# Two experts' reads, a third table and a new order of the first batch in a transformer layer with a mixture of experts

## What is computed

```python
x = x + tanh(g_xattn) * cross_attention(layernorm(x), ctx)   # 16 heads of 8, causal mask
x = x + tanh(g_ffn) * moe(layernorm(x))
# moe: 8 experts, each token takes its best 2
probs = softmax(xt @ Wr);  topv, topi = top_k(probs, 2);  topv /= topv.sum()
rank = cumsum(one_hot(topi), axis=0)          # place of a token with its expert
keep = (rank <= 160) * one_hot(topi)          # 160 = capacity, for each of the two choices
h = gelu(xt @ W1[e] + b1[e]);  y = h @ W2[e] + b2[e]     # 128 -> 512 -> 128, float32
out = sum over the token's kept choices of weight * y[e]
```

## Time and profile before

| | us |
|---|---|
| median of the runs (141.72 to 141.99) | 141.88 |
| the profiled execution | 142.43 |
| its span, first to last instruction | 140.2 |
| PE busy | 122.2 (87%) |
| DVE busy | 103.5 (74%) |
| POOL busy | 83.6 (60%) |
| ACT busy | 74.1 (53%) |
| POOL's 16 sends of rows (L558) | 18.6 |
| POOL's 18 scatters of results (L588) | 19.9 |

### The profile page before, as it was taken

One profiled execution on the slowest core, in us unless ns is written; L12 is line 12 of the kernel. 1 busy time (PEld: TensorE's weight loads), 2 busy tenths in 40 slices (PEclk: granted clock), 3 DMA queues, 4 the chain that ended last, 5 costly groups with the idle time before them and its releaser, 6 DMA issues.

```text
span 140.2 us, 2215 instructions
## 1 busy us (share of the span) xinstructions
PE 122.2 (87%) x698; PEld 85.1 (61%) x703; DVE 103.5 (74%) x262; ACT 74.1 (53%) x135; POOL 83.6 (60%) x125
## 2 busy tenths in 40 slices
PE   5998978999899999896989979969989999989920
PEld 2443844455455656633449647759889999967710
DVE  5599855947584637399569698793699999999290
ACT  4924667166361447335916397671697777811210
POOL 6679779999999140021678658760077877772000
PEclk9999999999999999999999999999999999999996
DMA  3899880003340000000079601113820001101805
GB/s 97 257 217 228 207 274 4 5 0 91 71 140 0 5 0 0 0 0 2 19 222 301 215 22 39 39 53 65 181 66 29 26 31 43 39 30 25 294 0 150
DMA packets 19017, 12.22 MB, mean 87 GB/s; under 512 B 3381, under 2 KB 16999, under 8 KB 19008
## 3 DMA queue, kind: packets, MB, share of 16 engines
q1 hardware_dynamic: 17344, 9.59, 26.7%
q0 software_dynamic: 1088, 1.86, 4.1%
q10 hardware_dynamic: 576, 0.66, 1.3%
HBM read 7.25 MB, written 5.06 MB: 88 GB/s over the span
## 4 chain that ended last, share of the span: by engine, by line
PE 27%; DVE 22%; POOL 17%; issue 15%; DMA 8%; ACT 6%; POOLq 2%; DVEq 0%; SPq 0%
PE turn L870 5%; POOL results L588 5%; DVE top L1319 5%; POOL slots L558 4%; DMA xn_all<-results 3%; PE turn L883 3%; PE av L926 3%; DVE shared L1621 3%; DMA X<-x 3%; POOL shared L479 2%; PE av L934 2%; PE turn L889 2%; DMA results<-p,result_of 2%; PE turn L1105 2%; PE sc L902 2%
## 5 line engine op out<-in xcount | busy, mean ns | idle before, releaser
L1319 DVE TENSOR_REDUCE top<-turn 128x3 fp32r<-128x462 f32 (+2 forms) x44 | 26.2, 606 | 13.6 <-PE turn L870 7.4
L588 POOL DMA_INDIRECT results<-p,result_of x18 | 19.9, 1103 | 13.6 <-DVE p L1604 8.4
L682 ACT ACTIVATE p_all<-sc 128x1024 f32<-128x1024 f32 x16 | 15.5, 1022 | 16.9 <-PE sc L902 16.9
L558 POOL DMA_INDIRECT slots<-rows,slot_of x16 | 18.6, 1164 | 9.3 <-issue 7.3
L870 PE MATMUL turn<-shared,q_all 128*128 128x462 f32 (+2 forms) x44 | 20.3, 468 | 2.3 <-DVE top L1319 0.8
L1196 PE MATMUL sc<-q_all,w_all 128*128 128x320 f32 x96 | 17.4, 320 | 1.1 <-issue 0.7
L756 ACT ACTIVATE late<-sc,B 128x320 f32<-128x320 f32 x32 | 14.9, 522 | 3.0 <-PE sc L1196 3.0
L1196 PEld LDWEIGHTS sc<-q_all,w_all 128*128 128x128 f32 x96 | 14.2, 188 | 2.2 <-issue 1.9
L870 PEld LDWEIGHTS turn<-shared,q_all 128*128 128x128 f32 x44 | 8.3, 189 | 11.2 <-ACT q_pack_all L645 3.8
L1621 DVE TENSOR_TENSOR shared<-late,shared 128x640 fp32r<-128x640 f32 x16 | 13.1, 821 | 0.3
L549 POOL TENSOR_SCALAR_AFFINE_SELECT p_all<-p_all 128x512 f32<-128x512 f32 x7 | 4.5, 644 | 9.5 <-ACT p_all L682 9.5
(11 more groups left out here) (252 smaller groups left out, 280.5 us busy)
## 6 DMA issues: line engine op xcount, KB each, us to landing
W<-w SPq DMA_DIRECT2D x8, 256.0 KB, 3.2
p_all<-w SPq DMA_DIRECT2D x8, 256.0 KB, 4.4
slots<-slot SPq DMA_DIRECT2D x1, 1386.0 KB, 10.6
results<-zeros SPq DMA_DIRECT2D x2, 512.0 KB, 9.3
parts_all<-slots SPq DMA_DIRECT2D x5, 198.0 KB, 3.0
X<-x SPq DMA_DIRECT2D x2, 256.0 KB, 3.6
xn_all<-results SPq DMA_DIRECT2D x2, 256.0 KB, 4.1
xn_all<-results ACTq DMA_DIRECT2D x2, 256.0 KB, 4.3
```

Source lines behind the costliest of these rows:

```text
L558: nc.gpsimd.indirect_dma_start(out=slots, out_offset=bass.IndirectOffsetOnAxis(ap=slot_of[:, c:c + 1], axis=0), in_=rows[:, t, :], in_offs ...
L588: nc.gpsimd.indirect_dma_start(out=results, out_offset=bass.IndirectOffsetOnAxis(ap=result_of[0:m, e, n:n + 1], axis=0), in_=y[0:m, e % 2, ...
L682: act.activation(p0[:, t, heads, :], sc[:, heads, :], ACT.Exp, scale=SCALE).then_inc(sc_free, 1)
L1319: dve.tensor_reduce(top[:, qt, h0:h0 + nh, 3 * HD], ps[:, 0:nh * keys].rearrange("p (h k) -> p h k", h=nh), AX.X, ALU.max).then_inc(turn_f ...
```

## The change

Expert 5's results go to a table of their own with one row per token, cleared by SP ahead of the third expert's weights. The table of the two choices is therefore complete after expert 4; SP reads it then, all four parts, and POOL adds the second choices to the first behind its last scatter. DVE adds these sums to x, then expert 5's rows, which SP and ACT read in halves. ACT takes every second store of the output, and the high parts of the last two experts' results. On DVE, expert 7's results come ahead of its second and third mark; on PE its turning comes ahead of most of expert 6's picks. In the first batch, choosing moves from group 5 to group 6, the three selections move forward, half of expert 2's gather takes the place of six fills, the values come ahead of projection and count, and POOL's root comes ahead of the eighth send. Cut to its core (semaphores and views left out):

```diff
-        SELECTED = {(0, 0): 1, (1, 0): 2, (0, 1): 3, (1, 1): 5, (2, 0): 6, (2, 1): 7}
+        SELECTED = {(0, 0): 1, (1, 0): 2, (2, 0): 3, (0, 1): 4, (1, 1): 6, (2, 1): 7}
@@ SP
             for e in range(E):
+                if e == 2:
+                    sp.dma_start(last_d, zeros[:, :].unsqueeze(1).to_broadcast([P, NT, D])).then_inc(last_laid, 16)
...
             for n in range(2):
-                sp.wait_ge(back[n], 16 * ST * STORED // 2)
-            for k in range(TOPK):
-                sp.dma_start(choice_rows[:, k, 0:QT], res_d[:, k, 0:QT]).then_inc(choice_in[k][0], 16)
+                sp.wait_ge(back[n], 16 * ST * (STORED // 2 - n))
+            for h in range(2):
+                for k in range(TOPK):
+                    tiles = slice(QT * h, QT * h + QT)
+                    sp.dma_start(choice_rows[:, k, tiles], res_d[:, k, tiles]).then_inc(choice_in[k][h], 16)
+            sp.wait_ge(h_split, 2 * E)
+            sp.wait_ge(last_back, 16 * ST)
+            sp.dma_start(last_rows[:, 0:QT], last_d[:, 0:QT]).then_inc(last_in[0], 16)
             n = NT // NPIECES
-            for c in range(NPIECES):
+            for c in range(0, NPIECES, 2):
@@ POOL
+            step(pool.memset(table_row[:, STORED - 1, :], 0.0))
...
-            for t in range(QT):
+            for t in range(QT - 1):
                 send(0, t)
+            send(0, QT - 1, range(TOPK - 1))
             root(blocks[1], 4)
+            send(0, QT - 1, range(TOPK - 1, TOPK))
...
+                table, places, landed = (results, TOPK * T, back[e % 2]) if e < STORED - 1 else (last_results, T, last_back)
+                if e == STORED - 1:
+                    pool.wait_ge(last_laid, 16)
...
+            for h in range(2):
+                tiles = slice(QT * h, QT * h + QT)
+                for k in range(TOPK):
+                    pool.wait_ge(choice_in[k][h], 16)
+                pool.tensor_tensor(choice_rows[:, 0, tiles], choice_rows[:, 0, tiles], choice_rows[:, 1, tiles],
+                                   ALU.add).then_inc(choices_added, 1)
@@ ACT
+            def high_results(e):
+                act.wait_ge(y_ready, e + 1)
+                act.activation(y_part[e - STORED][:, 0], y_last[:, e - STORED], ACT.Copy).then_inc(y_high, 1)
+            high_results(E - 2)
             add_bias(E - 1)
-            for n in range(2):
-                act.wait_ge(back[n], 16 * ST * STORED // 2)
-            for k in range(TOPK):
-                act.dma_start(choice_rows[:, k, QT:NT], res_d[:, k, QT:NT]).then_inc(choice_in[k][1], 16)
+            high_results(E - 1)
+            act.wait_ge(h_split, 2 * E)
+            act.wait_ge(last_back, 16 * ST)
+            act.dma_start(last_rows[:, QT:NT], last_d[:, QT:NT]).then_inc(last_in[1], 16)
...
+            for c in range(1, NPIECES, 2):
+                act.wait_ge(fin_ready, c + 1)
+                act.dma_start(out_d[:, n * c:n * c + n, :], fin[:, n * c:n * c + n, :]).then_inc(stored, 16)
@@ PE
+                if 1 <= g <= NG:
+                    values(g - 1)
                 if g == FIRST_TURNED:
                     for h in range(2):
                         project_first(h)
                 if g == FIRST_PLACED:
                     count(0)
-                if 1 <= g <= NG:
-                    values(g - 1)
...
-            fill(sc[:, 3, :], 4)
+            fill(sc[:, 3, :], 2)
             count(1)
-            fill(sc[:, 0, :], 8)
+            gather_on_chip(2, 0)
+            fill(sc[:, 0, :], 4)
...
             turn_results(0)
-            gather_on_chip(2, 0)
             gather_on_chip(2, 1)
...
             down(E - 1)
-            pick_results(E - 2, 0)
+            pick_results(E - 2, 0, range(1))
             turn_results(E - 1)
+            pick_results(E - 2, 0, range(1, ST))
             pick_results(E - 2, 1)
@@ DVE
-                if g == FIRST_TURNED:
+                if g == FIRST_PLACED:
                     choose(0)
-                if g == FIRST_PLACED:
                     dve.wait_ge(rstd_ready, 3)
                     scale_difference(0)
                     layernorm(blocks[0], x1, rows, rows_ready)
                     place(0)
+                    select_rows(0, 0)
                 if g == NG - 1:
                     last_later_keys()
-                    select_rows(0, 0)
+                    select_rows(0, 1)
                     low_of_rows(0, *blocks[0])
...
-            select_rows(0, 1)
+            select_rows(0, 2)
             choose_last()
...
-                dve.wait_ge(y_ready, e + 1)
-                step(dve.tensor_copy(y_part[i][:, 0], y_last[:, i]))
+                dve.wait_ge(y_high, i + 1)
...
             select_rows(1, 1, 2, QT)
-            select_rows(0, 2)
...
             mark_tokens(7, 0)
+            results_out(7)
             mark_tokens(7, 1)
+            split_results(7)
             mark_tokens(7, 2)
-            results_out(7)
-            split_results(7)
             for h in range(2):
                 tiles = slice(QT * h, QT * h + QT)
-                for k in range(TOPK):
-                    dve.wait_ge(choice_in[k][h], 16)
-                    step(dve.tensor_tensor(fin[:, tiles, :], fin[:, tiles, :], choice_rows[:, k, tiles], ALU.add))
+                dve.wait_ge(choices_added, h + 1)
+                step(dve.tensor_tensor(fin[:, tiles, :], fin[:, tiles, :], choice_rows[:, 0, tiles], ALU.add))
+            for h in range(2):
+                tiles = slice(QT * h, QT * h + QT)
+                dve.wait_ge(last_in[h], 16)
+                step(dve.tensor_tensor(fin[:, tiles, :], fin[:, tiles, :], last_rows[:, tiles], ALU.add))
```

More of the change, by code:

```diff
@@ L89, in build @@
         results = nc.dram_tensor("results", (TOPK * T, D), F32, kind="Internal").ap()
+        last_results = nc.dram_tensor("last_results", (T, D), F32, kind="Internal").ap()
         X = sb("X", [P, NT, D])
@@ L222, in build @@
             "p (e n d) -> p e n d", e=2, n=ST)
+        last_rows = late[:, 2 * QT * P:2 * QT * P + NT * D].rearrange("p (n d) -> p n d", n=NT)
         sumT = late[:, 0:2 * QT * P].rearrange("p (h q) -> p h q", h=2)
@@ L230, in build @@
                   for e in range(STORED, E)]
-        SELECTED = {(0, 0): 1, (1, 0): 2, (0, 1): 3, (1, 1): 5, (2, 0): 6, (2, 1): 7}
+        SELECTED = {(0, 0): 1, (1, 0): 2, (2, 0): 3, (0, 1): 4, (1, 1): 6, (2, 1): 7}
         def gathered(e):
-            return ((sc1, av)[e] if e < ON_CHIP else turn[e % 2])[:, 0:SLOTS]
+            return ((sc1, av)[e] if e < ON_CHIP else turn[(e + 1) % 2])[:, 0:SLOTS]
         def w1_whole(e):
@@ L298, in build @@
         back = [sem(f"back{n}") for n in range(2)]
+        last_back, last_laid, choices_added = sem("last_back"), sem("last_laid"), sem("choices_added")
+        last_in = [sem(f"last_in{h}") for h in range(2)]
+        y_high = sem("y_high")
         token_ready, pick_ready, y_split = sem("token_ready"), sem("pick_ready"), sem("y_split")
@@ L307, in build @@
         res_d = results.rearrange("(g p n) d -> p g n d", g=TOPK, p=P)
+        last_d = last_results.rearrange("(p n) d -> p n d", p=P)
         NPIECES = 4
@@ L588, in _ @@
                     nc.gpsimd.indirect_dma_start(
-                        out=results, out_offset=bass.IndirectOffsetOnAxis(ap=result_of[0:m, e, n:n + 1], axis=0),
+                        out=table, out_offset=bass.IndirectOffsetOnAxis(ap=result_of[0:m, e, n:n + 1], axis=0),
                         in_=y[0:m, e % 2, n, :], in_offset=None,
-                        bounds_check=TOPK * T - 1, oob_is_err=False).then_inc(back[e % 2], 16)
+                        bounds_check=places - 1, oob_is_err=False).then_inc(landed, 16)
+            for h in range(2):
[4 more added lines that the diff above has]
+                                   ALU.add).then_inc(choices_added, 1)
         @block.scalar
@@ L787, in _ @@
                 act.activation(sumT[:, h, :], turn[h][:, :], ACT.Copy).then_inc(sum_copied, 1)
+            n = NT // NPIECES
+            for c in range(1, NPIECES, 2):
+                act.wait_ge(fin_ready, c + 1)
+                act.dma_start(out_d[:, n * c:n * c + n, :], fin[:, n * c:n * c + n, :]).then_inc(stored, 16)
         @block.tensor
@@ L1074, in _ @@
                 maxima(maxima_beside(g, 3))
+                if g == 1:
+                    pe.wait_ge(v_ready, 5)
+                if 1 <= g <= NG:
+                    values(g - 1)
                 if g == FIRST_TURNED:
@@ L1100, in gather_on_chip @@
                 if e == ON_CHIP:
-                    pe.wait_ge(turn_free, full[0])
+                    pe.wait_ge(turn_free, use_of["fold", 2])
                 for part, ready in enumerate((rows_high, rows_split)):
@@ L1242, in _, with pick_results @@
                     down(e - 1)
-            def pick_results(e, h):
+            def pick_results(e, h, pieces=range(ST)):
                 pe.wait_ge(y_split, e - STORED + 1)
-                for n in range(ST):
+                for n in pieces:
```

(2 more changed lines are left out.)

4 lines of the change are left out of this document (1 added, 3 removed).

## The result

The changed kernel takes 140.7 (140.43 to 141.21, 6 runs) against 141.94 (141.58 to 142.32, 6 runs) for the kernel before: ratio 0.990 [0.986, 0.993]. That is faster by 1.2, with an interval that leaves out 1, where 2.7 was forecast. The profiled execution has a span of 138.6 instead of 140.2.

What follows compares the result with a forecast made beforehand. No single engine bounds it; one POOL queue sets two stretches, then a tail of scatter, read, eight adds, store. First batch 0.9 + 1.1 = 2.0, tail 0.2 + 0.5 = 0.7: 141.88 - 2.7 = 139.2, range 137.4 to 141.0.

Steps and rivals of the forecast that it cites:

- three signs that would show it wrong: Root staying at 78.6, first scatter staying at 102, or final adds waiting for expert 5's rows instead of GpSimd.
- Root one send earlier: POOL, first batch: root ahead of the eighth send could start at 77.36 instead of 78.63; gain 0.5 to 1.2, taken 0.9.
- the lost race: Rival, chance 0.25: the fifth send falls behind a selection, 1.4 late; root back at 78.7, time 140.1.
- Selection for expert 2's first half moved: DVE, first batch: moved from 85.62 into idle time, it frees a long send of 1.25 waiting; gain taken 1.1.
- The 0.61 of the earlier trace: DVE operation at 64.04 held by POOL; expected to start after POOL is done and take a fraction.
- Long send gone: POOL's second eight sends: the send of 2.22 at 85.73 would take 0.97; gain 0.5 to 1.25, taken 1.1.
- the slots' read gates the loop: Start of the experts' loop: slots arriving 2.0 earlier set its start; moving the gather and selection alone gains nothing.
- 0.2 for the adds: Tail: early reads and GpSimd's two adds, with DVE's own add held to 132.5; gain 0.2 to 1.8, taken 0.2.
- 0.5 for the stores: Output stores: with ACT taking every second one, the last store no longer starts 0.5 behind its piece.
- the clean adds: Rival, chance 0.20: GpSimd's adds slip past DVE undisturbed; tail 2.3, of which adds 1.8, time 137.6.
- the crowding: Rival, chance 0.05: early reads delay expert 5's last scatter, landing after 7.5, last reads taking 5.0; time 143.6, slower.
- The lock itself: Where POOL and DVE both read SBUF, the later waits for the other's end; sends ended 0.84 and 0.85 after selections.

Runs made afterwards that it cites:

- after_sel_late: The changed kernel with only the selection of expert 0 moved from behind the places to behind the last mask; 140.07, ratio 0.983.
- r6_values_later: root6 with PE's values put back behind the projection and the count; 138.93, ratio 0.974.
- after: The changed kernel itself, against the kernel before the change, in its first set of runs; 140.7, ratio 0.990.
- before: The kernel without the change, to which all ratios refer; 141.94 beside the first runs of the changed kernel.
- after_again: The changed kernel without an edit, measured a second time against the kernel before; 140.61, ratio 0.987.
- tail_only: The changed kernel with its first batch put back as before, so only the tail is changed; 141.59, ratio 0.996.
- r6_dve_adds: root6 with the adds of the choices on DVE again and none on GpSimd; 138.97, ratio 0.975.
- quarter_reads: The changed kernel with each of the four early reads cut to one of its four tiles, leaving results out; 139.98, ratio 0.983.
- root6: The changed kernel with POOL's root ahead of both sends of the fourth tile instead of the last send alone; 139.2, ratio 0.976.
- best2: root6 with expert 0's selection late, choices' adds on DVE, sums ahead of expert 5's rows, values behind projection and count; 137.3, ratio 0.963.

## Why the prediction was half right

Of the three signs that would show it wrong two came: the root stayed late (79.18), and the final adds waited for expert 5's rows instead of for GpSimd.

**Root one send earlier, 0.9: wrong in sign.** The root came 0.55 later. Seven sends took as long as eight had: first to root 10.79 instead of 10.99. I looked for the lost race at the fifth send; the one that lost was the second. The step that failed is "Selection for expert 2's first half moved ... the other two one place forward", where I asked only whether DVE had idle time for them. With a selection right behind the places the first send takes 1.59 (1.22 before, 1.45 with the selection later), and the send behind it starts 0.08 after the next selection's start (2.25, where 1.00 stood before). after_sel_late gives 0.8 of that back at the root. The rival of a lost race put the root at 78.7 and the time at 140.1; that is the case that came, by another send. The places themselves were 0.75 late, not 0.1: 0.39 of it is the price of the values ahead of projection and count, by r6_values_later; the other 0.35 differs between executions of one kernel: the row of PE's scores that starts at 20.60 in after starts at 20.27 in before and at 20.28 in after_again, where the root is 0.32 late. The 0.61 of the earlier trace rows did not vanish either: with the choosing moved, DVE's next operation (64.02, 0.67) meets the same POOL instruction (63.98, 0.63).

**Long send gone, 1.1: right in size, on a path that bound little.** The second eight got 1.27 shorter. But "the slots' read gates the loop" was too strong: the slots hold expert 3's up only through the gap behind DVE, by 0.45 in before (0.68 against the smallest, 0.23) and by 0.05 in after. tail_only has the long send (2.23) and no wait for the slots at all. What makes the wait long or short is how long the read takes from SP's first issue until DVE has the slots, 4.72 in before and at most 3.85 in tail_only, and that differs between executions of one kernel (4.41 in after, at most 3.80 in after_again). The lasting gain between root and expert 3, 0.99 on PE, comes from the part that I put at nothing: half of expert 2's gather off PE. The row that answers to the earlier trace rows is 95.02 with 1.17 instead of 2.35; 0.19 of it is lost again between the root and expert 0's up (6.68 instead of 6.49). The other half runs at 79.25, where the fills ran, ahead of a wait of PE for DVE. It needs its selection earlier, so moving the selection and moving the gather work together; neither was tried alone, and the sizes are read from rows. DVE's time without that selection behind expert 0's up brought nothing by itself: from expert 0's to expert 1's up it is 4.55 in both.

Sum of the first batch: 0.84 instead of 2.0, made of other terms than mine.

**Tail, 0.2 for the adds: right in size by luck; 0.5 for the stores: right** (0.55). From the last scatter to the last piece 0.21 was gained in after, but 0.62 in after_again and 0.65 in tail_only, as the scatter landed after 4.5 or 4.1. I took GpSimd's lock as the bound. The lock is there, but r6_dve_adds shows no cost of it. What keeps a quarter to a half of the clean adds' 1.8 away is the crowding that I gave one chance in twenty: the scatter lands after 4.1 to 4.6 beside the reads, 2.5 with a quarter of their bytes, and quarter_reads ends 0.42 to 0.83 sooner; behind it PE's sums are next. Its price was 1.6 to 2.1, not the 5.0 of that rival, so it took the gain and no more. Expert 7's new order and the high parts on ACT, put at nothing, were not tried alone. The Trainium skill (DMA: Bandwidth & Descriptors, "Queues, rings and completion order") has the engines take turns between queues packet by packet. No run here shows such turns: the scatter landed as the last early read did in after, and in after_again, tail_only and root6 too SP's issue behind the scatter comes within 0.14 of the GpSimd add behind that read. The 7.5 of the rival took the reads to start with the scatter; they had started 1.8 before it.

**The lock itself held**: 0.84 from the selection's end to the send's end again, at 72.54. The Trainium skill (SBUF — State Buffer, "SBUF: two separate sides") names a DVE operation in a two-port mode as what starves descriptors; the selection, with two inputs and 1.49 for 1280 elements, held POOL's indirect transfers in each of these traces, and the measurement decides.

## What to carry to other kernels

Before counting what a shorter queue gives, follow the chain past its end: one engine's queue fed two paths here (root to PE, sends to slots). An earlier root came through 1:1 (root6); shorter sends behind it counted only as far as PE's gap behind the slots could shrink, 0.45 at most in before. A gap that the profile calls "issue" can be a wait at second hand: find the engine whose result is used next, and what that engine waited for. A long DVE operation that reads SBUF does not belong beside a train of POOL's transfers; where it must be there, its start against theirs counts, not whether DVE has room. A read that is made early runs beside the transfer that ends last: count its bytes against that landing.

## What the runs showed of the hardware that was not expected

- The experts' loop has two lengths. From expert 3's up to the last scatter it is 23.57 to 23.66 in ten of the traces and 24.28 or 24.29 in four, both for the same changed kernel (after 23.66, after_again 24.28). In after_again one scatter took 1.44, beside DVE's marks, where its counterpart in after took 0.91. The ten are the traces in which DVE waits for the slots (0.51 to 1.22), the four those in which it does not. So what slots in time gained at expert 3's up was lost again among the scatters in these four; how the one leads to the other is open.
- SP's issue of the same eight reads of the slots took 4.10 in most executions and 4.89 to 4.99 in three (before, r6_values_later, best2: 4.98, 4.89, 4.99). In all three the values stand behind projection and count, but so they do in tail_only, which took 4.10. Open as well.
- GpSimd's add of 128x512 takes 1.29 alone and up to 1.83 where it meets DVE, and DVE's mark of 0.74 takes 1.61 to 2.29 then: both pay.
